# Cross-attention and a 4-bit feed-forward on one core: the passage between the two stages rebuilt, with reordered loads and buffers

## The reference

```python
def rmsnorm(x, g): return x * rsqrt(mean(x * x, -1) + 1e-5) * g
def layernorm(x):  return (x - mean(x, -1)) / sqrt(var(x, -1) + 1e-5)

# x (16, 100, 512), ctx (16, 361, 256); 16 heads of 128
h = layernorm(x)
q = rmsnorm((h @ Wq).reshape(16, 100, 16, 128), gq)
k = rmsnorm((ctx @ Wk).reshape(16, 361, 16, 128), gk)
v = (ctx @ Wv).reshape(16, 361, 16, 128)
attn = softmax(einsum('bqhd,bkhd->bhqk', q, k) / sqrt(128))
x = x + einsum('bhqk,bkhd->bqhd', attn, v).reshape(16, 100, 2048) @ Wo

# each weight is a 4-bit code times a scale for each block of 32 values
Wg, Wu, Wd = dequant(gate), dequant(up), dequant(down)  # 4096x512, 4096x512, 512x4096
h = layernorm(x)
g, u = h @ Wg.T, h @ Wu.T
out = x + ((tanh(0.79788456 * (g + 0.044715 * g**3)) * g * 0.5 + g * 0.5) * u) @ Wd.T
```

## Time and profile before

| | |
|---|---|
| median of 3 runs | 2132.9 us (2132.24 to 2133.37) |
| profiled execution, its own time | 2130.98 us |
| its span, first to last instruction | 2129.1 us |
| PE busy | 2041.5 us (96%), 11840 matmuls |
| DVE busy | 1413.2 us (66%) |
| ACT busy | 966.7 us (45%) |
| POOL busy | 913.7 us (43%) |

### The profile page before, as it was taken

One profiled execution on the slowest core, in us unless ns is written; L12 is line 12 of the kernel. 1 busy time (PEld: TensorE's weight loads), 2 busy tenths in 40 slices (PEclk: granted clock), 3 DMA queues, 4 the chain that ended last, 5 costly groups with the idle time before them and its releaser, 6 DMA issues.

```text
span 2129.1 us, 33346 instructions
## 1 busy us (share of the span) xinstructions
PE 2041.5 (96%) x11840; PEld 1962.0 (92%) x11840; DVE 1413.2 (66%) x2936; ACT 966.7 (45%) x2122; POOL 913.7 (43%) x1042
## 2 busy tenths in 40 slices
PE   5999999999999999998999967999999999999999
PEld 5899899999898899997999867999999999999998
DVE  4777777787877777876877855555555555555554
ACT  3555455555555455554555523333333333333332
POOL 6766655532344333443333233444444444444441
PEclk9999999999999999999999988999999999999999
DMA  5344333423233233233232254000001000000001
GB/s 174 104 138 163 130 114 128 140 94 125 84 107 111 85 99 132 80 112 100 89 99 94 71 156 124 31 30 30 31 32 35 32 32 30 31 30 30 1 1 62
DMA packets 95268, 175.34 MB, mean 82 GB/s; under 512 B 15024, under 2 KB 51520, under 8 KB 93056
## 3 DMA queue, kind: packets, MB, share of 16 engines
q1 hardware_dynamic: 95104, 173.21, 25.1%
HBM read 138.18 MB, written 35.00 MB: 81 GB/s over the span
## 4 chain that ended last, share of the span: by engine, by line
PE 86%; DMA 4%; DVE 4%; POOL 2%; issue 2%; ACT 1%; SPq 1%; DVEq 0%; POOLq 0%; ACTq 0%
PE psum L272 64%; PE psum L308 5%; PE psum L332 3%; PE psum L355 3%; PE psum L361 3%; PE psum L356 3%; PE psum L340 3%; PE psum L403 2%; DMA ctx_raw<-in_ctx 1%; DMA head_w<-spill_so 1%; DMA xb<-in_x 1%; SPq L1277 1%; DVE work L879 1%; POOL k_ss L1099 1%; DVE k_ss L831 1%
## 5 line engine op out<-in xcount | busy, mean ns | idle before, releaser
L1071 DVE TENSOR_TENSOR sq<-psum,sq 128x400 f32<-128x400 f32 x128 | 73.5, 574 | 284.5 <-ACT sq L760 284.5
L272 PE MATMUL psum<-wk,ctxT_hi 128*122 128x512 f32 x768 | 242.3, 397 | 11.1 <-DVE wk L780 11.1
L650 ACT ACTIVATE work<-psum,stats,q_rstd 100x361 f32<-100x361 f32 x256 | 163.7, 650 | 195.0 <-DVE stats L870 195.0
L780 DVE TENSOR_TENSOR kaT_lo<-psum,kaT_hi 128x488 fp32r<-128x488 f32 (+2 forms) x384 | 216.0, 612 | 45.6 <-ACT kaT_hi L603 45.5
L1271 POOL TENSOR_TENSOR inter_lo<-act,inter_hi 128x400 fp32r<-128x400 f32 x128 | 135.4, 1058 | 182.8 <-ACT inter_hi L603 182.8
L603 ACT CAST kaT_hi<-psum 128x488 fp32r<-128x488 f32 (+2 forms) x384 | 178.9, 539 | 63.6 <-PE psum L340 61.3
L862 DVE TENSOR_REDUCE stats<-psum 100x2 f32<-100x722 f32 x128 | 115.7, 904 | 130.2 <-PE psum L308 130.2
L1099 POOL TENSOR_TENSOR k_ss<-k_ss,power 122x4 f32<-122x4 f32 x192 | 195.2, 1017 | 16.0
L1049 DVE SCALAR_TENSOR_TENSOR ysum<-psum,ysum 128x400 f32<-128x400 f32 x256 | 142.3, 571 | 70.1 <-PE psum L272 69.9
L758 ACT ACTIVATE sq<-psum 128x400 f32<-128x400 f32 x128 | 64.4, 503 | 263.9 <-PE psum L272 263.9
L272 PE MATMUL psum<-inter_hi,down_hi 128*128 128x400 f32 x512 | 175.6, 343 | 4.7 <-ACT x2T L620 4.7
(11 more groups left out here) (125 smaller groups left out, 5599.7 us busy)
## 6 DMA issues: line engine op xcount, KB each, us to landing
head_w<-spill_sq SPq DMA_DIRECT2D x48, 512.0 KB, 3.5
head_w<-spill_so SPq DMA_DIRECT2D x48, 512.0 KB, 3.6
wk<-spill_sk SPq DMA_DIRECT2D x12, 1024.0 KB, 4.9
wv<-spill_sv SPq DMA_DIRECT2D x48, 256.0 KB, 2.8
spill_sq<-head_w SPq DMA_DIRECT2D x16, 512.0 KB, 3.0
spill_so<-head_w SPq DMA_DIRECT2D x16, 512.0 KB, 3.0
ctx_raw<-in_ctxT SPq DMA_DIRECT2D x16, 361.0 KB, 4.0
head_raw<-in_Wq SPq DMA_DIRECT2D x16, 256.0 KB, 3.6
```

The source lines that it names most:

```text
L272: last = e.matmul(out, a_, b_, start=i == 0, stop=i == len(passes) - 1)
L650: e.activation(attn[h][:, 0:SKV], bank[3 + h][0:SQ, 0:SKV], ACT.Exp, bias=st[:, h:h + 1], scale=rq[:, i * QH + h:i * QH + h + 1], accum_ou ...
L780: e.tensor_tensor(dst, src, high.bitcast(F32), ALU.subtract).then_inc(S[sem], 1)
L1071: e.tensor_tensor(gsq[z][:, :], gate, gsq[z][:, :], ALU.mult).then_inc(S["arg"], 1)
```

## The change

**Buffers.** SBUF is laid out anew, so that the feed-forward's first buffers lie where attention's free up before the end. The tile `sign` is gone: the sign is written into `value`, so that a piece waits for POOL's `scaled` of two pieces before ahead of its first operation. `xT_raw` is gone: x2 is loaded into `xT[ch]_lo`, ACT casts from it to `hi`, and POOL (not DVE) subtracts in place, 128 x 1600. The last two output weights have tiles `final_w` of their own. `ysum` holds chunks 0 to 2, and chunk 3 is summed in `x1T`.

**Early decode.** Pieces 0 to 5, and the split of chunk 0 of x2, move into units 59 to 62. For DVE these are `decode(0)` at the end of 59, 1 at the end of 60, 2 in the middle of 61, 3 at its end, 4 in the middle of 62, 5 at its end.

**Last unit and passage.** The first gate and up products stand between the dependent steps of unit 63 and of the last outputs. The last group's norms go from PSUM straight into `xT[3]`, without DRAM. `down(0)` and `down(1)` come after them. Block 1's first four pieces are decoded in step m = 3.

**Loads and stores.** The codes are loaded in unit 58 and x2's chunk 0 in unit 59. The fourth context load of v = 2 moves behind the reloads of the unit, in units 2, 18, 34 and 50. The result leaves in 16 stores (128 x 400) where there were 4 (128 x 1600).

The diff, cut to this:

```diff
-        sign, mag = tensor(f, "sign", [P, 4 * P], I16), tensor(f, "mag", [P, 4 * P], I16)
+        mag = tensor(f, "mag", [P, 4 * P], I16)
...
-        xT_raw = tensor(f, "xT_raw", [P, DC, CT])
...
 tensor_program
+            u, quad = UNITS - 1, NQ - 1
+            last = (NG - 1) * GB
+            scores(u)
+            output(quad - 1, 3, 2)
+            half(0, 0, 0)
+            half(0, 0, 1)
+            transpose_attn(u)
+            e.wait_ge(S["x1"], 4 * quad)
+            half(0, 1, 0)
+            attend(u, 0)
+            attend(u, 1)
+            e.wait_ge(S["yTl"], 2 * u + 1)
+            half(0, 1, 1)
+            e.wait_ge(S["ex"], 4 * UNITS)
+            for h in range(QH):
+                value_of(quad, h, LAST_BANKS[h])
+            half(1, 0, 0)
+            for c in range(DC):
+                output(quad, c, LAST_BANKS[c])
+            half(1, 0, 1)
+            e.wait_ge(S["x1"], 4 * NQ)
+            for b in range(GB):
+                residual_transposed(last + b, LAST_BANKS[b])
+            for b, (m, z, k) in enumerate(((1, 1, 0), (1, 1, 1), (2, 0, 0), (2, 0, 1))):
+                half(m, z, k)
+                e.wait_ge(S["xn2"], last + b + 1)
+                norm_transposed(last + b, 2, LAST_BANKS[b])
+            half(2, 1, 0)
+            half(2, 1, 1)
+            e.wait_ge(S["x3h"], GB)
+            e.wait_ge(S["x3l"], GB)
+            down(0)
+            down(1)
+            for m in range(3, STEPS):
+                gate_up(m)
+                down(m - 1)
+            down(STEPS - 1)
...
 scalar_program
+                if u == UNITS - 4:
+                    split_x(0)
                     decode_hi(0)
+                elif u == UNITS - 3:
+                    decode_hi(1)
+                    decode_hi(2)
+                elif u == UNITS - 2:
+                    decode_hi(3)
+                    e.wait_ge(S["k"], 3 * UNITS)
+                    decode_hi(4)
...
 vector_program
+                val = value[piece % 2]
...
+                if piece > 1:
+                    e.wait_ge(S["scaled"], piece - 1)
+                e.tensor_scalar(val[:, :], codes, 8 << 4 * nibble, 12 - 4 * nibble, ALU.bitwise_and,
                                 ALU.logical_shift_left).then_inc(dec, 1)
...
-                if piece > 1:
-                    e.wait_ge(S["scaled"], piece - 1)
...
+                if u in (UNITS - 3, UNITS - 2):
+                    decode(2 * (u - UNITS) + 8)
                 attended(u, 0)
...
+                if u >= UNITS - 5:
+                    decode((0, 1, 3, 5)[u - UNITS + 5])
...
 gpsimd_program
+            def split_x(ch):
+                e.wait_ge(S["xTh"], ch + 1)
+                e.tensor_tensor(xT[ch][1][:, :, :], xT[ch][1][:, :, :].bitcast(F32), xT[ch][0][:, :, :].bitcast(F32),
+                                ALU.subtract).then_inc(S["xTl"], 1)
...
+                elif u == UNITS - 3:
+                    split_x(0)
+                    decode_scaled(2)
+                    decode_lo(1)
+                    decode_scaled(3)
...
+            decode_lo(4)
+            decode_lo(5)
+            inter_lo(0)
+            split_x(1)
+            inter_lo(1)
+            split_x(2)
+            inter_lo(2)
+            for b in range(GB):
+                ln_rstd(2, last + b)
...
 sync_program
-                if v == 2:
-                    load_ctx_after("N", g * GB + 2)
...
                 for n in used_in(u):
                     if n + 2 not in FRESH_PLACE and n + 2 < len(ITEMS):
                         reload_head(n + 2)
+                if v == 2:
+                    load_ctx_after("N", g * GB + 2)
...
+            e.wait_ge(S["sc"], 4 * UNITS)
             load_x2(1)
+            load_final(2)
+            e.wait_ge(S["aTp"], UNITS)
+            load_final(3)
+            e.wait_ge(S["y"], 2 * UNITS)
             for ch in range(NCHUNK - 1):
                 load_y(ch)
+            load_codes(1)
+            e.wait_ge(S["o"], 4 * NQ)
+            load_x2(2)
...
             for ch in range(NCHUNK):
+                for c in range(DC):
+                    e.wait_ge(S["yadd"], 4 * (NCHUNK * (JT - 1) + ch) + c + 1)
+                    load(d["out"][:, c, cols(ch, CT)], residual(ch, c), f"d_o{ch}")
```

More of the change, by code:

```diff
@@ L445, in tensor_program @@
             squares_summed(0, QH - 1, 5)
-            for u in range(UNITS):
+            for u in range(UNITS - 1):
                 quad, i = u // GB, u % GB
@@ L450, in tensor_program @@
                 scores(u)
-                if u + 1 < UNITS:
-                    for t in range(KT):
-                        keys(u + 1, t)
+                for t in range(KT):
+                    keys(u + 1, t)
                 if i == 0 and quad > 0:
@@ L559, in down, with half @@
-            def down(jt, ch):
-                m = NCHUNK * jt + ch
+            def half(m, z, k):
+                jt, ch = m // NCHUNK, m % NCHUNK
+                n = 2 * m + z
+                if ch == 0 and z == 0:
+                    e.wait_ge(S["wh"], PIECES * jt + 2 * k + 2)
+                    e.wait_ge(S["wl"], PIECES * jt + 2 * k + 2)
+                if jt == 0 and z == 0 and k == 0 and ch < NCHUNK - 1:
+                    e.wait_ge(S["xTh"], ch + 1)
+                    e.wait_ge(S["xTl"], ch + 1)
+                if n > 1:
+                    e.wait_ge(S["inter" if k else "gelu"], n - 1)
+                wh, wl = (t[:, :].rearrange("p (c n) -> p c n", c=DC) for t in weight[k][jt % 2])
+                ns = cols(z, P)
+                matmul3(bank[2 * z + k][:, 0:CT],
+                        [(wh[:, c, ns], wl[:, c, ns], xT[ch][0][:, c, :], xT[ch][1][:, c, :])
+                         for c in range(DC)]).then_inc(S[("gate", "up")[k]], 1)
@@ L561, in down, with gate_up @@
+            def gate_up(m):
+                for z in range(2):
+                    for k in range(2):
+                        half(m, z, k)
+            def down(m):
+                jt, ch = m // NCHUNK, m % NCHUNK
                 if ch == 0:
@@ L1052, in last_norms @@
-            def last_norms(step):
-                j, part = (NG - 1) * GB + step // 3, step % 3
-                if part == 0:
-                    ln2_moments(j)
-                elif part == 1:
-                    ln2_normalise(j)
-            for m in range(STEPS):
-                jt, ch = m // NCHUNK, m % NCHUNK
+            u, quad = UNITS - 1, NQ - 1
+            last = (NG - 1) * GB
+            for p in range(2):
+                maxima(u, p)
+                negated(u, p)
+            add_output(quad - 1, 2, 7)
@@ new lines, in vector_program @@
+            argument(2)
+            add_output(quad, 0, LAST_BANKS[0])
+            gelu(2)
+            for c in range(1, DC):
+                add_output(quad, c, LAST_BANKS[c])
+            gated(2)
+            ln2_moments(last)
+            ln2_moments(last + 1)
+            ln2_normalise(last)
+            ln2_moments(last + 2)
+            ln2_normalise(last + 1)
+            argument(3)
+            norm3_lo(0)
+            ln2_moments(last + 3)
+            ln2_normalise(last + 2)
+            gelu(3)
@@ L1061, in vector_program @@
+            gated(3)
+            norm3_lo(1)
+            ln2_normalise(last + 3)
+            argument(4)
+            norm3_lo(2)
+            gelu(4)
+            gated(4)
+            norm3_lo(3)
+            argument(5)
+            gelu(5)
+            gated(5)
+            down_add(0)
+            decode(PIECES)
+            down_add(1)
+            decode(PIECES + 1)
+            for m in range(3, STEPS):
                 for z in range(2):
                     n = 2 * m + z
-                    gate, up = bank[2 * z][:, 0:CT], bank[2 * z + 1][:, 0:CT]
@@ L1084, in vector_program @@
-                if m > 0:
-                    down_add(m - 1)
+                    argument(n)
+                    for piece in pieces_at(m, z):
+                        decode(piece)
+                    gelu(n)
+                    gated(n)
+                down_add(m - 1)
             down_add(STEPS - 1)
@@ L1268, in gpsimd_program @@
                         decode_scaled(piece)
[L1269 to L1271 removed]
+                    inter_lo(2 * m + z)
                 if ch == NCHUNK - 1 and jt + 1 < JT:
```

463 lines of the change are left out of this document (219 added, 244 removed).

## The result

The changed kernel takes 2113.07 us (median of 4 runs, 2111.3 to 2116.02) against 2133.14 us: the ratio is 0.9903, interval 0.9886 to 0.9921. That is 20 us faster, where I had forecast 31 us. The time lies outside my own case (2092 to 2110 us) and 1 us inside the upper end of the range (2114 us). The profiled execution took 2116.02 us with a span of 2114.2 us, 14.9 us shorter than the earlier trace rows.

What follows compares the result with a forecast made beforehand. PE was taken as the bound, with only its waits and the low clock behind them to win. Terms -42.7 + 2.9 + 4.4 - 16.1 + 22.6 - 2.0 = -30.9 us gave a 2102 us median; range 2081 to 2114 us.

Steps and rivals of the forecast that it cites:

- my own case: Whole kernel: the prediction's terms hold as summed, giving 2092 to 2110 us; chance 62%.
- The passage: Last unit's scores to end of third `down`: 116.5 us falls to 73.8 us if no wait stays, -42.7 us.
- The wait for chunk 2: In the passage: x2's chunk 2 lands late behind residual loads and codes; PE waits 1.4 us plus clock, +2.9 us.
- Units 61 and 62: POOL's split holds DVE's `decode(2)`; PE waits 2.4 us, loses clock: +4.4 us (+1.3 us if holds are at most 1.2 us).
- The reload: Output-weight reload no longer queued behind the fourth context load: PE's 6.28 us wait goes, again one group later, -16.1 us.
- The late context: Units 3, 19, 35, 51: moved context load takes 9.3 us, lands after PE wants it, +22.6 us.
- Rival A: At the moved place context loads land fast, so their 22.6 us cost becomes 0 to 2 us: 2080 us; chance 15%.
- The tail: PE's end to span's end: last store has 200 KB in place of 800 KB and lands sooner, -2.0 us.
- step 3: Feed-forward step with four decode pieces: extra DVE and POOL work taken as 0, upper bound 4 us.
- Rival B: The passage keeps waits at hand-overs, eight places costing 8 to 20 us: 2110 to 2120 us; chance 18%.
- Rival C: PE's passage waits only move, for instance to late `x2` or codes; all 42.7 us go: 2130 to 2136 us; chance 3%.
- Rival D: Feed-forward steps slow as DVE decode operations meet POOL's: 60 steps of 1.2 us, 2174 us; chance 2%.

## Why the prediction came out 11 us off

**The passage, -42.7 us: right.** Without its one wait it takes 74.0 and 73.7 us in two kernels, where the sum of its work was 73.8 us.

**The wait for chunk 2, +2.9 us: right in place and cause, too small.** It cost 81.6 - 73.97 = 7.7 us, 4.8 us more. The term that was mis-sized is the landing. I had it 33.2 us after the unit's scores (1251.3 less 1218.1), and it was 1277.1 - 1240.2 = 36.9 us. I took 380 GB/s for the residual loads and the chunk and 7 us for the codes. In the trace the rate was below that, with the DMA engines' share at its full value:

```profile
1262.00:1266.00 4.00, 4.00 (x24) 4.00 (x23) 1.30 (x3) 1.54 (x3) 0.25 (x1) 1.00 1.07 329
1270.00:1274.00 4.00, 4.00 (x24) 4.00 (x23) 1.15 (x2) 0.00 (x0) 0.00 (x0) 1.00 1.05 222
```

SP issues the next block's codes right behind the chunk, but there is no sign that those had a part in its 15 us: with both blocks' codes issued behind it, it landed in 4.9 us. The wait itself is 5.65 us where I had 1.4 us, and the low clock behind it (granted 0.50 from 1284 to 1290 us) makes up the other 2.0 us, where I had 1.4 us.

**Units 61 and 62, +4.4 us: right**, +4.7 us, with the wait 2.92 us where I had 2.4 us and the held operation 3.32 us where I had 2.5 us. The value from "at most 1.2 us are a hold", the lower one in the prediction, is refuted.

**The reload, -16.1 us: right, too large by 2.8 us.** The waits went. But in unit 34 a wait for `ctxN_lo` of 1.05 us, 0.15 us before, took a part of their place, and the granted clock of the unit was 0.93. Unit 50 has nearly the same wait (0.88 us) at 1.00, and missed by 0.4 us only. So most of the 2.8 us goes with the low clock in unit 34.

**The late context, +22.6 us: right, too small by 2.5 us.** The load took 9.4 us in unit 35 where I had taken 9.3 us. The distribution was off: unit 3 lost 6.8 us (7.9), and unit 19 8.3 us (4.9), where further waits for the keys' normalisation followed, since POOL did the split of a weight (1.9 us) and then the keys' 1/rms behind the context. I had put these "in the same waits"; in unit 19 they were not. Rival A, at 15%, falls: in the place it spoke of the load took 9.4 us.

**The tail, -2.0 us, and step 3, 0: right**, -1.9 us and -0.1 us. Rival B, many small waits at hand-overs, falls as well: there is none. Rival C, waits that only move, falls with the 35 us. Rival D falls with the feed-forward, which takes the same 789 us.

**The sum.** The misses on the terms (4.8 + 0.3 + 2.8 + 2.5 + 0.1 = 10.5 us, less 0.1 us in step 3) turn -30.9 into -20.5 us, and the medians differ by 20.1 us. The profiled execution shows only -14.9 us, and the rest is ahead of unit 0. Only profiled executions have a trace, so that the others lack this stretch's 5 us is inferred. All these misses but the 0.1 us go the same way, and none hides another (within the late context, unit 3's 1.1 us took from unit 19's 3.4 us). They carried the time out of my own case, into the 2110 to 2120 us that I had given rival B, but not by B's mechanism. That it still lies in the range is luck as far as my terms go: the upper end was set by a part of B.

**Ahead of unit 0: open.** The stretch from the start to the first scores took 46.5 us in the kernel before and 51.7 us in the changed one. The work is the same, and so are the waits within 1 us; between 36 and 52 us the granted clock was 0.66:

```profile
36.00:52.00 16.00, 13.71 (x69) 13.31 (x70) 4.04 (x10) 5.82 (x12) 9.93 (x11) 0.66 0.68 223
```

In the kernel before the granted clock from 36 to 47 us was 1.00. In another kernel that is the same as the changed one up to there (the load between the reloads), 36 to 47 us has 0.95, and the stretch took 46.5 us, too:

```profile
36.00:47.00 11.00, 9.12 (x65) 8.67 (x65) 4.09 (x10) 5.05 (x11) 9.18 (x10) 0.95 0.80 244
```

The ten kernels of the study made from the changed one took 46.5 to 51.2 us there, two of them 46.5 us, and the three profiles of the kernel before and its variants 46.5 to 46.6 us. So it looks to be mostly an execution's own, at the low clock or not, and not a cost of the change that I could show. Whether the new order of the buffers makes the low clock more frequent is open: three profiles of the one kind are too few.

## What to carry to other kernels

Cost what a moved DMA itself takes at the new place, and not only what it was holding up: this one freed 13 us and cost 25 us. Look first at why the transfer is slow, since its shape (112 and 10 rows in place of 122) won as much on the old kernel as the whole change. And in an in-order queue ask what stands behind each instruction that waits for a DMA: the one wait left in the passage went by moving two small operations past it, or the load past the codes.

## What the runs showed of the hardware that I had not expected

- A transfer of 122 x 2 x 256 fp32 with a second one of 117 x 256 took 9.4 us, and 4.4 us when the first went as 112 and 10 rows. For 4 us of the slow one the 16 DMA engines' busy share was 0.14.
- An integer operation of 128 x 512 on DVE, 0.41 us alone, took 3.32 us beside one POOL instruction of 3.62 us, and 0.75, 1.27 and 1.14 us in a row beside four of about 1.15 us each. Each of the three ended 0.28 us behind one of the four, so cutting the POOL instruction moves the hold more than it removes it.
- The same first 50 us of a program ran at a granted clock of 0.66 (a mean of the two levels, 1.2 and 2.4 GHz) or 0.95 in their last part, which goes with 5 us.
